# A spiking RWKV layer with a split-precision feed-forward on one core: one count for two layers' spikes, a scan source in PSUM, other orders on four engines

## The reference

```python
x = x + LN(attn_block(LN(x)))
x = x + LN(ffn(LN(x)))
```

## Time and profile before

| | |
|---|---|
| median of 3 runs | 667.36 us (666.34 to 667.45) |
| the profiled execution: its own time | 668.46 us |
| its span, first to last instruction | 666.3 us |
| mean granted TensorE clock | 0.966 |
| TensorE / VectorE / ScalarE / GpSimd busy | 588.5 / 565.4 / 535.1 / 412.5 us |

### The profile page before, as it was taken

The page is one execution under the profiler, slowest core; times in us unless marked ns, Lnnn a source line. Parts: engine busy times, 40 slices in busy tenths (PEclk is TensorE's granted clock), DMA queues, the critical chain, the costliest instruction groups (busy, mean ns, idle before and its releaser), DMA issues. The chain is left out here.

```text
span 666.3 us, 9752 instructions
## 1 busy us (share of the span) xinstructions
PE 588.5 (88%) x2241; PEld 364.2 (55%) x2241; DVE 565.4 (85%) x1532; ACT 535.1 (80%) x849; POOL 412.5 (62%) x576
## 2 busy tenths in 40 slices
PE   1366699999999999999999999999999999999982
PEld 0122256575655656565656656565756565656661
DVE  2968888999999999999999999989899889875532
ACT  5666788979797988979797988979797988957662
POOL 3453446577767677677667677776837663464453
PEclk9759799999999999999999999999999999999997
DMA  8010000000010101010010101010000101000001
GB/s 287 1 32 16 18 17 16 17 27 7 17 33 17 32 17 32 17 33 0 17 33 17 31 18 31 17 32 17 24 10 0 33 1 32 1 16 2 16 1 31
DMA packets 26558, 17.02 MB, mean 26 GB/s; under 512 B 1152, under 2 KB 25728, under 8 KB 26240
## 3 DMA queue, kind: packets, MB, share of 16 engines
q1 hardware_dynamic: 26496, 16.34, 8.0%
HBM read 12.14 MB, written 4.19 MB: 25 GB/s over the span
## 5 line engine op out<-in xcount | busy, mean ns | idle before, releaser
L2231 PE MATMUL p_f<-a_lo,w_hi 128*128 128x512 f32 x320 | 135.0, 422 | 7.9 <-DVE a_lo L287 6.9
L902 ACT ACTIVATE hid<-p_f,scale 128x512 f32<-128x512 f32 x128 | 87.9, 687 | 61.0 <-PE p_f L2231 60.4
L2231 PE MATMUL p_f<-a_hi,w_hi 128*128 128x512 f32 x320 | 125.8, 393 | 0.0
L2231 PE MATMUL p_f<-b_lo,w_hi 128*128 128x512 f32 x256 | 111.6, 436 | 2.8 <-DVE b_lo L287 1.3
L2231 PE MATMUL p_f<-b_hi,w_hi 128*128 128x512 f32 x256 | 100.6, 393 | 0.0
L896 ACT ACTIVATE a_hi<-hid 128x512 fp32r<-128x512 f32 x128 | 78.7, 630 | 10.6 <-DVE hid L1636 9.1
L426 POOL TENSOR_TENSOR nd<-factors,pq 128x512 f32<-128x512 f32 x32 | 38.3, 1196 | 71.3 <-DVE pq L1503 71.3
L287 DVE TENSOR_TENSOR a_lo<-hid,a_hi 128x512 fp32r<-128x512 f32 x96 | 74.9, 798 | 7.4 <-ACT a_hi L896 6.5
L2231 PEld LDWEIGHTS p_f<-a_lo,w_hi 128*128 128x128 f32 x320 | 60.3, 188 | 31.7 <-ACT a_hi L896 12.7
L410 POOL TENSOR_TENSOR rstd<-var,minus_half 128x4 f32<-128x4 f32 x64 | 69.6, 1092 | 1.6
L287 POOL TENSOR_TENSOR a_lo<-hid,a_hi 128x512 fp32r<-128x512 f32 x32 | 48.0, 1499 | 30.2 <-ACT a_hi L896 30.0
(11 more groups left out here) (141 smaller groups left out, 1448.7 us busy)
## 6 DMA issues: line engine op xcount, KB each, us to landing
xa<-in_x SPq DMA_DIRECT2D x16, 256.0 KB, 2.8
xb<-in_x SPq DMA_DIRECT2D x16, 256.0 KB, 3.0
out<-y_out SPq DMA_DIRECT2D x16, 256.0 KB, 3.3
kk<-in_ffn SPq DMA_DIRECT2D x1, 1024.0 KB, 7.2
hid<-in_ffn SPq DMA_DIRECT2D x1, 1024.0 KB, 9.8
mix<-in_mix SPq DMA_DIRECT2D x1, 512.0 KB, 6.4
gate<-in_ffn SPq DMA_DIRECT2D x1, 512.0 KB, 5.8
mix<-in_mix SPq DMA_DIRECT2D x1, 320.0 KB, 3.8
```

Source lines behind the costliest of these rows:

```text
L902: act.activation(hid[:, m], p_f[m % 2][:, :], ACT.Gelu, scale=scale[:, 1 + layer, m:m + 1]).then_inc(s_gelu[layer], 1)
L2231: last = pe.matmul(out_, w[:, b], x[:, k], start=(k == 0 and t == 0), stop=(k == n - 1 and t == len(terms) - 1))
```

## The change

1. `bv` keeps one of its two halves. `terms(g, 1)` writes its product over v in the PSUM bank `p_v`, and `sum_over_time(g, 0)` scans it there. `terms(g, 0)` comes first. TensorE's writers of `p_v` (`to_gate(g, 1)`, and `v_product` in the opening) now wait for the end of the second scan (`after(pe, s_pq, n, 2, 2)`) and no longer for `s_bv[0]`.
2. The counts of neuron 0 of group n and neuron 1 of group n-1 stand side by side: one `fired_sum(g)`, one `fired_flags(g)`, one semaphore. There are 17 rounds where there were 32.
3. The last group's norm and residual move from GpSimd to VectorE (`last_norm`, `last_sum`), and its result is stored in two halves.
4. The lists of calls of all engines are ordered anew, in `opening`, `turn` and `ending`.

```diff
-        bv = sb("bv", [P, 2, NB, T])
+        bv = sb("bv", [P, NB, T])
...
-        fired = [sb(f"fired{k}", [P, 1], BF16) for k in range(2)]
-        fired_all = [sb(f"fired_all{k}", [P, 1]) for k in range(2)]
+        fired = sb("fired", [P, 2], BF16)
+        fired_all = sb("fired_all", [P, 2])
...
-                pool.wait_ge(s_fired_all[k], g.n + 1)
+                pool.wait_ge(s_fired_all, g.n + 1 + k)
...
                 dve.wait_ge(s_expB, g.n + 1)
                 dve.wait_ge(s_v, g.n + 1)
-                dve.tensor_tensor(flat(bv[:, n]), flat(factors[:, 2 + n]), p_v[:, :], ALU.mult).then_inc(s_bv[n], 1)
+                if n == 1:
+                    dve.wait_ge(s_bv[0], g.n + 1)
+                dve.tensor_tensor(p_v[:, :] if n else flat(bv[:, :, :]), flat(factors[:, 2 + n]), p_v[:, :], ALU.mult).then_inc(s_bv[n], 1)
 
             def sum_over_time(g, n):
 
...
                 wait(dve, s_apq, 2 * g.n)
                 if n == 0:
                     dve.wait_ge(s_bv[1], g.n + 1)
-                new = factors[:, 3] if n else bv[:, 1]
+                new = factors[:, 3] if n else p_v[:, :].rearrange("p (b t) -> p b t", b=NB)
                 for b in range(NB):
                     last = dve.tensor_tensor_scan(pq[:, n, b, 1:T + 1], factors[:, 1, b], new[:, b], 0.0,
                                                   ALU.mult, ALU.add)
...
             def numerator(g):
                 dve.wait_ge(s_bv[0], g.n + 1)
                 dve.wait_ge(s_apq, 2 * g.n + 2)
-                dve.tensor_tensor(nd[:, 0], nd[:, 0], bv[:, 0], ALU.add).then_inc(s_num, 1)
+                dve.tensor_tensor(nd[:, 0], nd[:, 0], bv[:, :, :], ALU.add).then_inc(s_num, 1)
 
             def ratio(g):
                 dve.wait_ge(s_num, g.n + 1)
...
                 wait(dve, s_spikes[k], g.n)
                 fed = flat(h_in[k][:, :, :]) if k else p_k[:, :]
                 dve.tensor_scalar(flat(spikes[k][:, :, :]), fed, 0.5, None, ALU.is_ge, ALU.add,
-                                  accum_out=fired[k][:, :]).then_inc(s_fired[k], 1)
-
-            def fired_flag(k, g):
-
-                dve.wait_ge(s_fired_sum[k], g.n + 1)
-                wait(dve, s_spikes[k], g.n)
-                dve.tensor_copy(fired_all[k][0:1, :], p_m[0][0:1, 2 * k:2 * k + 1]).then_inc(s_fired_all[k], 1)
+                                  accum_out=fired[:, k:k + 1]).then_inc(s_fired[k], 1)
+
+            def fired_flags(g):
+
+                dve.wait_ge(s_fired_sum, g.n + 1)
+                wait(dve, s_spikes[0], g.n)
+                wait(dve, s_spikes[1], g.n - 1)
+                dve.tensor_copy(fired_all[0:1, :], p_m[0][0:1, 0:2]).then_inc(s_fired_all, 1)
...
+            def last_norm(g, h):
+
+                dve.wait_ge(s_shift5, g.n + 1)
+                dve.wait_ge(s_rstd[5], g.n + 1)
+                for j in (2 * h, 2 * h + 1):
+                    last = dve.tensor_scalar(f_out[:, j], f_out[:, j], rstd5[:, j:j + 1], shift5[:, j:j + 1], ALU.mult,
+                                             ALU.add)
+                last.then_inc(s_last_n, 1)
+
+            def last_sum(g, h):
+
+                dve.wait_ge(s_last_n, h + 1)
+                wait(dve, s_stored, 16 * g.n)
+                dve.tensor_tensor(y_out[:, 2 * h:2 * h + 2], f_out[:, 2 * h:2 * h + 2],
+                                  xres[:, g.par, 2 * h:2 * h + 2], ALU.add).then_inc(s_last_out, 1)
+
...
-                if i >= 4:
+                if 4 <= i < GROUPS + 3:
                     store(G[i - 4])
-            sp.wait_ge(s_stored, 16 * GROUPS)
+            for h in range(2):
+                sp.wait_ge(s_last_out, h + 1)
+                sp.dma_start(out_tiles[GROUPS - 1][:, 2 * h:2 * h + 2],
+                             y_out[:, 2 * h:2 * h + 2]).then_inc(s_stored, 16)
+            sp.wait_ge(s_stored, 16 * (GROUPS + 1))
...
-                def fired_sum(k, g):
-
-                    pe.wait_ge(s_fired[k], g.n + 1)
-                    pe.matmul(p_m[0][:, 2 * k:2 * k + 1], ones16[:, :], fired[k][:, :], start=True,
-                              stop=True).then_inc(s_fired_sum[k], 1)
+                def fired_sum(g):
+
+                    if g.n < GROUPS:
+                        pe.wait_ge(s_fired[0], g.n + 1)
+                    wait(pe, s_fired[1], g.n)
+                    pe.matmul(p_m[0][:, 0:2], ones16[:, :], fired[:, :], start=True, stop=True).then_inc(s_fired_sum, 1)
```

More of the change, by code:

```diff
@@ L307, in build @@
         FIRST, LAST = 5, 12
-        G = [Group(n) for n in range(GROUPS)]
+        G = [Group(n) for n in range(GROUPS + 1)]
         def groups(i):
@@ L924, in opening @@
                 high_weights(0)
+                high_weights(2)
                 tanh_1(G[0])
-                high_weights(3)
-                under(G[0], 1)
-                bounds(G[0])
-                exp_table()
-                exps(G[0], 0)
-                under(G[0], 0)
-                exps(G[0], 1)
-                norm_1(G[1])
+                under(G[0], 1)
+                under(G[0], 0)
+                exp_table()
+                exps(G[0], 1)
+                bounds(G[0])
+                exps(G[0], 0)
+                norm_1(G[1])
+                high_weights(3)
                 log(G[0])
                 inverse(G[0])
-                high_weights(2)
                 z_1(G[1])
@@ L950, in opening @@
                 exp_table()
+                exps(G[1], 1)
                 exps(G[1], 0)
-                exps(G[1], 1)
+                rest_weights(2)
+                square(G[0], 0)
                 relu(G[0], 1)
-                norm_1(G[2])
-                square(G[0], 0)
                 square(G[0], 1)
@@ L985, in opening @@
                 silu(G[0], 1)
-                square(G[1], 3)
+                norm_1(G[3])
                 high(1, G[0], 0)
-                z_1(G[3])
                 silu(G[0], 2)
@@ L1281, in ending @@
                 inverse(G[15])
+                square(G[14], 3)
                 silu_table()
@@ L1821, in turn @@
                 excess(g[1])
+                mix_1(g[1], 2)
                 norm_2(g[2])
@@ L2302, in opening @@
                     channel_v(G[0], 1)
-                    after(pe, s_z2, G[0].n)
-                    turn_1(G[2])
                     channel_v(G[0], 2)
```

972 lines of the change are left out of this document (477 added, 495 removed).

## The result

The changed kernel took 671.25 us (median of 5 runs, 670.16 to 672.30), the kernel before beside it 667.36 (666.29 to 669.23). The ratio is 1.0057, with a 95% interval of 1.0043 to 1.0072: 0.6% slower, where I had forecast 9.9 us less. The profiled execution has a span of 669.1 us against 666.3.

The account below looks back on a forecast made before the run. Two nearly full engines, TensorE and VectorE, handing over to each other were taken to bound the turn. Turns -6.4, opening -0.8, ending -1.5, last group -1.1 gave -9.8 on 668.46: 658.7, median 657.5 us; range 650 to 668.

Parts of the forecast that it names:

- TensorE's 0.68 us for `a_lo`: In each turn, TensorE's wait behind VectorE's blocked `a_lo`; its removal was credited as -0.7 us a turn.
- the credit of 0.2 a turn: In the turn, `mix_1(g[1], 2)` ahead of `n2` brings `mixed2` earlier, using TensorE's 0.17 us wait: -0.2 us.
- Rival B: In the turn, the block moves from `a_lo` to VectorE's `yr`: +0.9 us a turn, 672.7 us; chance 0.18.
- Rival C: At `to_gate(g, 1)`, TensorE waits for the later second scan, losing the turn's gain: 666 us; chance 0.08.
- -0.8 a turn, eight turns -6.4: The loop's sum: -0.7 for `a_lo`, -0.2 for `mixed2`, +0.1 for `f_cm`, over eight turns, in us.
- the long `a_lo`: VectorE's `a_lo` of block 0, 1.76 us behind GpSimd's against 0.68, said to stand once in every turn.
- priced 0.1: In the turn, `output_scaled` behind one more `square` delays `f_cm`: +0.1 us, upper bound +0.57.
- The opening: Ahead of the first `yr`, `low_weights(3)` leaves the chain: -0.8 us taken of 0.93, first `yr` near 31.5 us.
- Joint counts, 0: 15 count rounds go; VectorE's saved 0.15 us copy already lies inside another credit, so counted 0.
- Product and scan in PSUM, 0: In the recurrence, moving product and scan to PSUM bounded by +-0.05 us an instruction, taken as 0.
- Last group, -1.1: At the end, norm and sum on VectorE take 2.1 us against GpSimd's 3.17; second store 1.1 us earlier.
- Ending, -1.5: In the groups after the loop, half of a turn's gain for some four groups: -1.5 us.

Follow-up runs that it names:

- e5: Changed kernel with TensorE's branch early, VectorE's second-layer low half moved back, and first norm's variance ahead of GpSimd's third-layer low half again: 660.52 us.
- e6: Changed kernel with the recurrence's second product written to SBUF again and scanned there, all orders kept: 671.54 us.
- e4: Kernel before, with TensorE's register load and branch moved late, right ahead of the first gate product: 671.97 us.
- e1: Changed kernel with TensorE's register load and branch back at their old place behind the third group's k product: 668.63 us.
- e9: Changed kernel with the edits of e1 and e2 together; the third-layer pair still runs beside GpSimd: 664.76 us.
- e2: Changed kernel with VectorE's second-layer low half, `low(2, g[4], 1)`, back behind the third norm's statistics: 667.56 us.
- e11: Changed kernel with the edits of e2 and e3, the branch left late: 665.0 us.
- e7: Kernel before, with only the last group's final scaling and addition on VectorE in halves, each stored by its own DMA: 666.29 us.
- e8: Kernel before, with only joint fired counts, one product and one copy for both neurons, placed behind the later threshold where needed: 677.14 us.
- e12: e10 with the second product in SBUF, scanned ahead of the first product in group 2, and `p_v` rewritten once both products are read: 661.09 us.
- e10: e5 with two more VectorE moves: `f0(G[0])` ahead of `terms(G[2], 0)`, `low(2, G[13], 3)` ahead of `stats_2(G[15])`: 661.11 us.
- e3: Changed kernel with first norm's variance ahead of GpSimd's third-layer low half again, and its moments moved ahead on VectorE: 669.92 us.

## Why the prediction was wrong

**The turn.** Most of what I took out went: TensorE's 0.68 us for `a_lo`, the 0.41 for `n`, the idle time ahead of `n2`. The wait for `mixed2` did not: it is 1.3 us in the eight turns before, 1.2 after, and the credit of 0.2 a turn that I gave for it never came. Rivals B and C did not happen at their places. What failed is the step from there to "-0.8 a turn, eight turns -6.4"; the eight turns became 0.6 us longer. I credited the waits that go and priced only those moves of the new turn that touch them; `variance(1, g[0])` leaving its place ahead of GpSimd's `low(3, g[4], 0)`, and `low(2, g[4], 1)` going ahead of `add_2`, stood in the order of both kernels and got no price. Each makes a new pair of the kind that I had just read from the earlier trace rows: 0.81 us for `kk` and up to 0.92 for `b_lo`. The first of them could be seen in the kernel before: I wrote that the long `a_lo` stands once in every turn, and in the turn that ends at the first row there is a second, at 298.67. With both undone (e5) the turn is 36.55 and the eight take 6.0 us less than before, close to what I had credited. In part that is luck in the terms: beside the `mixed2` that did not come, the wait for `f_cm` is 3.7 us in e5's eight turns against 1.1 before, 0.3 a turn where I had priced 0.1, and 3.0 us for GpSimd's `b_lo` had no place in my sum. Rival B was the right mechanism, looked for at the one op that the diff moved next to the old block, and not at every VectorE op with two SBUF inputs whose neighbour on GpSimd had changed. That its figure, 672.7, is 1.5 us from the measured time is luck: it had +0.9 a turn, and what was measured is +0.07 a turn and a loss in the opening. The Trainium skill (SBUF — State Buffer, the section on who interferes with whom) puts it generally: the port pair is held for a whole instruction by whichever starts first, and a VectorE instruction needs it where two of its inputs are in SBUF. The runs agree, 0.68 alone and 1.76 to 1.81 behind a GpSimd op; the scan with one input in PSUM was not blocked, 1.26 against 1.67. Below a lead of 0.08 us the recorded starts don't say who was first: at 0.03 VectorE was blocked at 361.55, GpSimd in e6 at 136.75.

**The opening.** "-0.8" held as far as I walked it: the first `yr` came at 31.1 (I had written 31.5). The step that failed is that I let this stand for the whole opening. I stopped there, and 50 us further on lay the largest single loss, 4.9 us between groups 1 and 2. Nowhere had I named the register load and branch; the trace of before shows them only as part of a 3.18 us wait that has another cause. Its price is measured from both sides: +4.8 us in the kernel before (e4), -2.6 in the changed one (e1), 2.8 with the second-layer block gone (e9 against e2), 4.5 in the repaired one (e11 against e5). At the last `yr` of the profiled executions, ahead of the ending's spells of clock, these four are 4.2, 2.0, 3.4 and 3.4. The Trainium skill had the warning (Runtime: NRT & Kernel Launch, the section on instruction fetch mechanics): a taken branch whose target is not in the window fetched ahead stalls for a fetch. What part of the 2.8 to 3.4 us is the load and what the fetch, no run here tells. Even with the branch early, group 2 comes 30.85 us after group 1 (28.8 in e7): some 2 us of the relaid opening, with a TensorE wait of over 4 us for the third input of group 2 at 68 to 70 us in every kernel of the new order, is left, and I did not settle what in it costs them. Whether the joint count has a share, e8 doesn't show: its group 2 comes 29.2 us after group 1.

**Joint counts, 0.** Right in the loop (298.3 us against 298.4), wrong as a statement on the part: it needs neighbouring thresholds, and outside the loop costs 3 to 4 us at each of the two places where they are not.

**Product and scan in PSUM, 0.** Right: +22 and -30 ns an instruction by the means, e6 and e12 without a difference that can be measured. The reason that I gave was a misreading: the 704 of the earlier trace rows is no price of an SBUF source, the median is 677, and the rest is two blocked scans in the opening. The figure of the Trainium skill (VectorE: DVE Perf Modes, the section on the TRN2 errata) I applied to three operations; only the two scans change their source, since the product reads `p_v` in both kernels. By it they would cost, as an estimate, 0.13 us a turn and e6 would have been some 2 us shorter than the changed kernel; it was 0.3 longer, and the measurement decides against that figure for this case. Rival C's wait is there once in the changed kernel, 0.21 us, and in e10 with 0.81 us, all ahead of the loop's turns. Its 666 also lacked the step from the profiled execution to the median that the other sums have.

**Last group, -1.1.** Mechanism right, size low: 1.75 between shift and end, in e7 too (6.2 to 4.4); e7's time gives 0.6 to 2.2. The second store is issued 2.2 us after the last shift, as written (2.1), but before it was 3.6, not the 3.17 that I counted from the norm's start; and the half store lands some 0.3 us sooner (2.2 us from issue to the end, before 2.6).

**Ending, -1.5.** -0.9 up to the last `yr`; behind it nothing is left of the last group's 1.75, the execution shown has a spell of low clock there (below). The range, 650 to 668, failed because B, the only slower case, was a single place and a single mechanism, while losses from places not walked had no share.

## What to carry to other kernels

When one blocked pair is resolved by laying an order anew, go through *every* op of either engine that shares the port and ask who starts first now, in ties most of all: one moved line is enough to bring the block back at another pair. In its mean duration a group of instructions hides a few blocked ones; its median and maximum show them. A register load and branch on TensorE belongs where the engine waits for something else anyway, and such a place has to be kept when the order around it changes. And a gain counted from waits that go is an upper bound until each moved step has been given a price.

## What the runs showed that I had not expected

**An uncovered branch often costs more than its idle time.** Six profiled executions have the branch late (the changed kernel, e2, e3, e4, e6, e11); TensorE stands idle for 2.8 to 3.4 us in all of them, and in all but e6 some microseconds at 1.2 GHz follow between 84 and 92 us, with matmuls of 0.63 us for 0.39. The eight without that idle time were granted 2.4 GHz from 84 to 92. In e6 group 2's `yr` came at 91.12, in the changed kernel at 92.31, in e1 at 89.91: of the 2.4 us that e1 gained there, roughly half is idle time and half clock. These are single executions, whose `yr` of group 1 already lie up to 0.9 us apart, so the split is an estimate.

**The same idle time, with and without a drop.** In the ending TensorE waits 1.77 us for `b_lo` in all kernels of the new order but e10 and e12. Some executions then show the low clock and some don't. Stretches of the changed kernel:

```profile
588.00:592.00 4.00, 1.82 (x7) 1.22 (x8) 2.85 (x16) 0.51 (x2) 2.21 (x6) 0.98 0.11 31
592.00:596.00 4.00, 4.00 (x15) 3.17 (x13) 3.23 (x16) 1.45 (x3) 0.94 (x1) 0.60 0.00 0
```

and of e1:

```profile
592.00:596.00 4.00, 4.00 (x18) 3.13 (x17) 3.61 (x13) 3.52 (x6) 3.15 (x4) 1.00 0.00 0
```

From the last `yr` to the end, the executions with the drop take 93.2 to 93.3 us (the changed kernel, e6, e9, e11), those without 91.4 to 92.1 (e1, e2, e3, e5, e10, e12): 1.1 to 1.8 us that no edit made. The 4.2 and 4.5 us between e5 and e9 or e11 may contain some of it. A good part of the spread in the times of one kernel may be this; I did not test it.

**A tie makes turns of two lengths.** With the two `b_lo` starting within 0.3 us of each other, one and the same program had turns of 36.8 and 37.8 us one after another, in the changed kernel, e1 and e6; with the tie resolved (e2, e5) they repeat to within 0.1 us from the third to the seventh.
